# Residual kept feature-major in SBUF, expert layer norms by block transposes, routers in plain float32

## The chip, the cores and the metric

One core of one Trainium2 chip runs the whole program in one launch. The metric is the device time in microseconds. The kernel before took 512.14 us (median of 3 runs, 511.82 to 512.53).

## What is computed

A transformer block in float32 on x of shape (4, 512, 256): four batches of 512 tokens with 256 features. Cut to what matters:

```python
x = x + tanh(g_xattn) * attention(layernorm(x), ctx, ctx)   # 16 heads of 64, rope, window of 64
x = x + tanh(g_ffn)   * experts(layernorm(x))

def attention(q, k, v):             # per batch
    qh, kh, vh = rope(q @ wq.T), rope(k @ wk.T), v @ wv.T
    scores = where(window, qh @ kh.T * 64**-0.5, -1e30)
    return softmax(scores) @ vh @ wo.T

def experts(x):                     # 2 shared and 16 routed experts of width 128
    shared = sum(gelu(x @ up.T) @ down.T)
    probs = softmax(x @ router_w.T); gate = top 4 of probs, else 0
    routed = sum(gelu(x @ up.T) * gate @ down.T)
    return shared + routed
```

## The kernel before

All large products are made from float32r pairs: each operand is split into a high part (rounded by ScalarE, ACT) and a low part (the rest, subtracted by VectorE, DVE, or GpSimd, POOL), and `product` (L1126 to L1134) issues three matmuls on TensorE (PE) for a pair: high x high, high x low, low x high. In the names, xTh and xTl are the two parts of the normalised input with features on partitions, oTh and oTl those of the attention output (and of the experts' hidden values), wh and wl those of the weights, which come in pieces of 512 columns through four raw buffers.

The program runs in two phases. Attention goes through 16 units u (4 batches b of 4 groups g of 4 heads), and each unit through 4 chunks c, one per head; `steps` (L204 to L236) lists for each chunk the jobs that go with it: "q", "k", "v" project the next unit, "y" of unit u - 1 multiplies its attention output by wo and adds it to x, "w" fetches and splits a weight piece. Each engine walks the same list in order: PE makes scores, transposes probabilities and multiplies by v; DVE takes score maxima (L1026), inverts sums (L1036), makes the low parts (rest_att, L1040), rotates q and k (L856, L859), adds y (L962); ACT makes exponentials (L707) and copies; POOL does half of the rotation (L499 to L513), divides the probabilities (`divide`, L521) and makes some low parts of weights. The PSUM banks `ring[0]` and `ring[1]` alternate between the jobs q, k, v, y, xT and r.

x lies token-major, as (128 tokens, batch, 4 tiles, 256 features). For y the stationary operand is a tile of 128 tokens of oTh or oTl, and the moving operand is 256 columns of wo: 4 tiles x 2 head pairs x 3 = 24 matmuls (L1249 to L1258).

The expert phase runs through 4 x 18 steps n = (b, e): PE computes up(n) (6 matmuls of 512 columns into ring[0]) and down(n - 2) (6 matmuls; they accumulate over the 18 experts of a batch), ACT applies gelu (L616) and rounds (L632), DVE multiplies by the gate (`gated`, L921) and makes the low part (`rest_gated`, L929). `after` (L243 to L259) lists the extra jobs behind each expert: weight pieces in the first batch, and the preparation of the next batch.

That preparation, for the experts' layer norm of batch b: "stat" (DVE bn_stats L820, bn_aggr L823, L825, L826; POOL takes the power -0.5 at L555 and the shift at L556), "norm_a" and "norm_b" (ACT, L697) into xn; then for batches 0 and 1 "xT": PE transposes xn in 8 matmuls (L1219), ACT rounds the bank (L604, L606), DVE makes the low part (L804, L807). For batches 2 and 3 "turn": DVE transposes 32x32 blocks (L992), and 16 DMAs a time on SP's queue (`move`, L373) bring the blocks to their partitions; "xhi" and "xlo" split. Then "r" (router): batches 0 and 1 multiply a split router weight `rw_parts` by xTh and xTl in four matmuls of 512 columns (L1273), batches 2 and 3 (`FULL_ROUTER`) multiply in plain float32 in 8 matmuls of 128 columns (L1263). "rexp", "pick_a", "pick_b", "gT" and "spread" make the gates and broadcast them through DRAM. "back" turns x itself feature-major (L1005 and 16 DMAs), and "z" adds the experts' sum to it (L1014); the store follows. The layer norm ahead of attention uses for batches 0 and 1 the same token-major way, for batches 2 and 3 a second, feature-major input `in_xt` scaled on POOL (L540, L546).

What orders the work: on each engine the program's order, written out by hand, and semaphores between engines. After attention's steps a closing part (L1096 to L1117 on DVE, L1375 to L1393 on PE) mixes the last chunks with the first experts.

## Time and profile before

| | us |
|---|---|
| median of 3 runs | 512.14 |
| lowest, highest | 511.82, 512.53 |
| the profiled execution | 510.9 |
| its span in the profile | 509.1 |

Busy time is given for each engine: PE matmuls, PEld weight loads (beside the matmuls), DVE, ACT, POOL. In rows of a timeline the columns are the start, the duration, the engine, the line, the operation with its tiles and shapes, how many were merged, and in brackets the idle time of the engine just before with what ended it. Durations of neighbours on DVE and PE overlap, since an instruction begins while the one before drains: for a pace, starts are compared. Step 53 and the like are values of c.

### The profile page before, as it was taken

Reading aid. Unit: us, or ns where it says so; the run is one execution under the profiler, and the core shown is the slowest. Engines: PE = TensorE matmul, PEld = TensorE weight load, DVE = VectorE, ACT = ScalarE, POOL = GpSimd, SP = SyncE. Lnnn points to the kernel's source line nnn. Section 1 sums busy time; section 2 is a strip of 40 time slices with the busy share of each in tenths; the row PEclk is TensorE's granted clock in tenths of the full one; section 3 lists DMA queues with packets and bytes.
Section 4 is the critical chain, followed back from the end, with each engine's and each line's share of the span. In section 5 each row is a group of like instructions: output and inputs, shape, how many; then the busy total and the mean of one; then the engine's idle time right before and its main releaser. Section 6 shows DMA issues by size and latency. Waiting matters only on the chain.

```text
span 509.1 us, 12348 instructions
## 1 busy us (share of the span) xinstructions
PE 499.7 (98%) x4402; PEld 420.1 (83%) x4402; DVE 358.1 (70%) x1159; ACT 310.7 (61%) x861; POOL 266.8 (52%) x206
## 2 busy tenths in 40 slices
PE   8998999999999999999999999999999999999997
PEld 5788888889988998888888788777878887888885
DVE  6989958665787667767977777796657565745454
ACT  5596785656766665765876775766456545544442
POOL 4999999899997999997897511001000100000000
PEclk9999999999999999999999999999999999999999
DMA  7463224121123201220220147315701580256021
GB/s 264 120 203 65 58 69 131 43 80 38 46 75 78 62 27 34 57 58 9 74 59 23 38 138 259 103 27 169 251 14 29 151 266 14 32 144 241 1 34 49
DMA packets 49355, 46.23 MB, mean 91 GB/s; under 512 B 29936, under 2 KB 32368, under 8 KB 49296
## 3 DMA queue, kind: packets, MB, share of 16 engines
q1 hardware_dynamic: 49296, 45.46, 31.4%
q8 instruction: 35, 0.57, 0.5%
q14 instruction: 24, 0.20, 0.2%
HBM read 32.72 MB, written 2.24 MB: 69 GB/s over the span
## 4 chain that ended last, share of the span: by engine, by line
PE 79%; POOL 9%; DVE 5%; issue 3%; ACT 2%; DMA 1%; SPq 0%; DVEq 0%; POOLq 0%; ACTq 0%
PE ring L1131 56%; PE psS L1131 10%; PE psO L1341 5%; PE psS L1310 4%; PE psT L1322 4%; POOL prob L521 2%; POOL arena L508 2%; POOL arena L513 2%; DMA craw<-in_ctx 1%; POOL wl L529 1%; POOL arena L502 1%; DVE arena L859 1%; DVE arena L1026 1%; DVE wl L946 1%; DVE arena L856 1%
## 5 line engine op out<-in xcount | busy, mean ns | idle before, releaser
L1131 PE MATMUL ring<-xTh,wh 128*128 128x512 f32 x268 | 108.1, 403 | 0.3 <-DVE lex L888 0.2
L1131 PE MATMUL ring<-xTh,wl 128*128 128x512 f32 x268 | 105.2, 393 | 0.0
L1131 PE MATMUL ring<-xTl,wh 128*128 128x512 f32 x268 | 105.1, 392 | 0.0
L632 ACT ACTIVATE oTh<-prob 128x512 fp32r<-128x512 f32 x64 | 40.4, 632 | 54.4 <-PE ring L1131 26.8
L521 POOL TENSOR_TENSOR prob<-prob,rinv 128x512 f32<-128x512 f32 x62 | 66.7, 1076 | 13.0 <-DVE rinv L1036 12.9
L929 DVE TENSOR_TENSOR oTl<-prob,oTh 128x512 fp32r<-128x512 f32 x64 | 44.1, 689 | 37.1 <-ACT oTh L632 36.6
L555 POOL TENSOR_TENSOR rstd<-vare,mhalf 128x4 f32<-128x4 f32 x8 | 9.7, 1212 | 103.2 <-DVE vare L826 103.2
L616 ACT ACTIVATE sneg<-ring 128x512 f32<-128x512 f32 x72 | 42.9, 595 | 33.1 <-PE ring L1131 33.0
L921 DVE TENSOR_TENSOR prob<-sneg,arena 128x512 f32<-128x512 f32 x64 | 44.2, 690 | 24.8 <-ACT sneg L616 24.8
L1131 PEld LDWEIGHTS ring<-xTh,wh 128*128 128x128 f32 x268 | 50.3, 188 | 12.7 <-issue 0.9
L1131 PEld LDWEIGHTS ring<-xTh,wl 128*128 128x128 f32 x268 | 50.3, 188 | 11.1
L1131 PEld LDWEIGHTS ring<-xTl,wh 128*128 128x128 f32 x268 | 50.4, 188 | 10.4
L723 ACT ACTIVATE pT<-psT 128x512 f32<-128x512 f32 x64 | 38.0, 594 | 33.4 <-PE psT L1322 33.2
L707 ACT ACTIVATE prob<-arena,nmax 128x128 f32<-128x128 f32 x128 | 49.7, 394 | 10.9 <-DVE nmax L1026 10.8
L707 ACT ACTIVATE prob<-sneg,nmax 128x128 f32<-128x128 f32 x128 | 49.6, 391 | 6.8 <-DVE nmax L1026 6.7
L513 POOL TENSOR_TENSOR arena<-arena 128x512 f32<-128x512 f32 x37 | 48.9, 1322 | 2.7
L508 POOL TENSOR_TENSOR arena<-arena,sin 128x512 f32<-128x512 f32 x37 | 50.1, 1353 | 0.0
L856 DVE STREAM_SHUFFLE arena<-ring 128x512 f32<-128x512 f32 (+1 forms) x51 | 45.8, 897 | 0.2
L859 DVE TENSOR_TENSOR arena<-ring,cos 128x512 f32<-128x512 f32 (+1 forms) x51 | 41.3, 809 | 0.0
L729 ACT ACTIVATE oTh<-psO 128x512 fp32r<-128x512 f32 x32 | 19.1, 597 | 33.1 <-PE psO L1341 33.0
L962 DVE SCALAR_TENSOR_TENSOR x<-ring,tg,x 128x1024 f32<-128x1024 f32 x16 | 20.5, 1278 | 26.4 <-PE ring L1131 26.4
L1131 PE MATMUL ring<-wh,oTh 128*128 128x256 f32 x128 | 37.4, 292 | 1.5 <-DVE oTl L1040 1.4
(144 smaller groups left out, 1247.7 us busy)
## 6 DMA issues: line engine op xcount, KB each, us to landing
arena<-gate_scratch SPq DMA_DIRECT2D x64, 256.0 KB, 6.1
raw<-in_e SPq DMA_DIRECT2D x18, 256.0 KB, 2.6
raw<-in_w SPq DMA_DIRECT2D x16, 256.0 KB, 3.6
arena<-arena SPq DMA_DIRECT2D x16, 256.0 KB, 3.2
arena<-arena SPq DMA_DIRECT2D x16, 192.0 KB, 3.5
pT<-pT SPq DMA_DIRECT2D x96, 32.0 KB, 2.0
out<-x SPq DMA_DIRECT2D x16, 128.0 KB, 6.0
x<-in_x SPq DMA_DIRECT2D x3, 512.0 KB, 4.4
```

The source lines that it names most:

```text
L508: link(pool.tensor_tensor(part, part, sin[:, :], ALU.mult))
L513: pool.tensor_tensor(dst, dst, swap[:, i, pair, :], ALU.add).then_inc(qk_rot[i], 1)
L521: pool.tensor_tensor(prob[:, c % BUFS, :, :], prob[:, c % BUFS, :, :], rinv[:, c % BUFS, :].unsqueeze(2).to_broadcast([P, TT, P]), ALU.mul ...
L616: act.activation(act_g[:, n % 2, :], ring[0][:, n % 2, :], ACT.Gelu).then_inc(f_gelu, 1)
L632: act.activation(gated_parts(n)[0], src, ACT.Copy).then_inc(f_hi, 1)
L707: last = act.activation(prob[:, c % BUFS, t, :], sneg[c % BUFS][:, t, :], ACT.Exp, bias=nmax[:, c % 4, t:t + 1], scale=-1.0, accum_out=rsu ...
L723: act.activation(pT[:, c % 4, :, :], psT[:, :, :], ACT.Copy).then_inc(p_out, 1)
L856: dve.stream_shuffle(swap[:, i, pairs, :], part, [(lane + QUAD // 2) % QUAD for lane in range(QUAD)]).then_inc(qk_swap[i], 1)
L859: dve.tensor_tensor(dst[:, pairs, :], part, cos[:, :].unsqueeze(1).to_broadcast(part.shape), ALU.mult).then_inc(qk_mul[i], 1)
L921: dve.tensor_tensor(act_f[:, n % 4, :], act_g[:, n % 2, :], gate_bc[:, r, :], ALU.mult).then_inc(f_mul, 1)
L929: dve.tensor_tensor(lo, src, hi.bitcast(F32), ALU.subtract).then_inc(f_lo, 1)
L1131: last = pe.matmul(out, a, b, start=start and i == 0 and j == 0, stop=stop and i == n - 1 and j == 2, skip_group_check=check)
```

## The change

- x is kept feature-major, as (128 features, batch, 2 halves, 512 tokens), loaded from the second input `in_xt` for all batches (semaphores `in_xd`). The token-major copy goes only to xn, for the norm ahead of attention; ACT then normalises xn in place.
- y is computed with the weights stationary: 2 halves of features x 2 head pairs x 3 = 12 matmuls whose moving operand is 512 columns of oTh or oTl. z adds to x in place; "back" of before and all block moves by DMA go.
- The experts' layer norm works on x turned by 32x32 blocks: in such a tile each of 4 partition quadrants holds, for a block of 32 tokens, a quarter of the features along the free axis. Jobs, one batch at a time: "turn" (DVE transposes x into xn), "mean" (DVE reduces over two axes, copies the four quadrants' sums side by side, reduces them, spreads -mean to the quadrants in four operations), "centre" (POOL adds it, two operations), "square" (POOL, two), "var" (DVE, as mean, on the squares), "scale" (POOL: power -0.5 of 128x16, then two products), "back" (DVE transposes the blocks back). "xhi" and "xlo" split for all batches, and xT(4) and xT(5) go.
- For batch 0 these stand at steps 44 (turn), 46, 47, 51, 53 (var), 55, 57, 58 and 59; for the others behind experts e = 2 (turn), 3 (mean, centre), 4 (square), 5 (var), 6 (scale), 7 (back), 8, 9 of the batch before.
- All routers are in plain float32 (8 matmuls of 128 columns); `rw_parts` goes. The gates go to DRAM in four DMAs for every batch.

```diff
-            for e, kind in ((2, "turn"), (8, "xhi"), (9, "xlo"), (10, "r"), (11, "rexp"), (12, "pick_a"),
-                            (13, "pick_b"), (14, "gT")):
+        for b in range(B - 1):
+            for e, kind in ((2, "turn"), (3, "mean"), (3, "centre"), (4, "square"), (5, "var"), (6, "scale"), (7, "back"),
+                            (8, "xhi"), (9, "xlo"), (10, "r"), (11, "rexp"), (12, "pick_a"), (13, "pick_b"), (14, "gT")):
                 after[b * NE + e].append((kind, b + 1))
...
+            jobs += {44: [("turn", 0)], 46: [("mean", 0)], 47: [("centre", 0)], 51: [("square", 0)], 53: [("var", 0)],
+                     55: [("scale", 0)], 57: [("back", 0)], 58: [("xhi", 0)], 59: [("xlo", 0)]}.get(c, [])
...
                 elif kind == "q" and n % GROUPS == 0 and n // GROUPS + 1 < B:
                     b = n // GROUPS + 1
-                    sp.dma_start(x[:, b, :, :], x_d[b]).then_inc(in_x[b], 16)
+                    if b == 1:
+                        sp.dma_start(x[:, 0, :, :], xt_d[0]).then_inc(in_xd[0], 16)
+                        load_tokens(b)
+                    sp.dma_start(x[:, b, :, :], xt_d[b]).then_inc(in_xd[b], 16)
                     load_ctx(b)
...
+            def feature_norm(kind, n):
+                if kind == "centre":
+                    pool.wait_ge(f_mean, n + 1)
+                elif kind == "square":
+                    pool.wait_ge(f_centred, n + 1)
...
+                else:
+                    pool.wait_ge(f_var, n + 1)
+                    link(pool.tensor_tensor(rstd_d[:, :], vare_d[:, :], mhalf_d[:, :], ALU.pow))
+                for k in range(KC):
+                    half = xn_halves[:, k, :, :]
+                    if kind == "square":
+                        flat = xd[:, k, :]
+                        last = pool.tensor_tensor(turned(n)[:, k, :], flat, flat, ALU.mult)
+                    else:
+                        values, op = (nmean_d, ALU.add) if kind == "centre" else (rstd_d, ALU.mult)
+                        last = pool.tensor_tensor(half, half, per_block(values), op)
...
+            def over_features(halves):
+
+                link(dve.tensor_reduce(part[:, :], halves.rearrange("p k m d -> p m k d"), AX_XY, ALU.add))
+                for a in range(4):
+                    last = dve.tensor_copy(four[:, :, a], part[QUAD * a:QUAD * (a + 1), :])
+                link(last)
+                link(dve.tensor_reduce(total[:, :], four[:, :, :], AX_X, ALU.add))
...
+                elif kind == "mean":
+                    over_features(xn_halves)
+                    for a in range(4):
+                        last = dve.tensor_scalar(nmean_d[QUAD * a:QUAD * (a + 1), :], total[:, :], -1.0 / D, None,
+                                                 ALU.mult)
+                    last.then_inc(f_mean, 1)
+                elif kind == "var":
+                    dve.wait_ge(f_squared, n + 1)
+                    over_features(turned(n).rearrange("p k (m d) -> p k m d", m=BLOCKS))
...
+                elif kind == "back":
+                    dve.wait_ge(f_scaled, n + 1)
+                    dve.transpose(turned(n).rearrange("p k n -> p (k n)"), xn_flat).then_inc(f_turned, 1)
...
-                    for t in range(TT):
-                        last = product(two[t // 2][:, (t % 2) * D:(t % 2 + 1) * D],
-                                       [(oTh[:, j, t * P:(t + 1) * P], oTl[:, j, t * P:(t + 1) * P])
-                                        for j in range(2)],
-                                       [cols(i, j * D, D) for j in range(2)])
+                    for kc in range(KC):
+                        last = product(two[kc], [cols(i, j * D + kc * P, P) for j in range(2)],
+                                       [(oTh[:, j, :], oTl[:, j, :]) for j in range(2)])
```

## Rows read from the trace of the kernel before

**Rows 1.** The page: busy us, share of the span and instructions.

```profile
PE 499.7 (98%) x4402; PEld 420.1 (83%) x4402; DVE 358.1 (70%) x1159; ACT 310.7 (61%) x861; POOL 266.8 (52%) x206
```

**Rows 2.** Busy time by stretch, then granted clock, DMA share, GB/s.

```profile
30.00:87.00 57.00, 54.67 (x683) 47.90 (x685) 46.59 (x175) 42.61 (x147) 55.90 (x43) 1.00 0.36 94
300.00:340.00 40.00, 40.00 (x216) 32.23 (x214) 30.04 (x63) 26.13 (x47) 1.70 (x2) 1.00 0.50 159
```

**Rows 3.** The chain of waits: start, us, what (k, then y).

```profile
109.44 2.76 PE ring L1131 x12
...
118.26 2.88 PE ring L1131 x24
```

**Rows 4.** Timeline of PE: transposes of xT(4), and a plain router.

```profile
281.60 1.03 PE L1219 MATMUL ring<-ident,xn 128*128 128x128 f32 x8
282.47 0.60 PE L1322 MATMUL psT<-ident,prob 128*128 128x128 f32 x4
...
381.04 0.63 PE L1263 MATMUL psT<-pT,rw 128*16 128x128 f32 x16
381.60 0.50 PE L1131 MATMUL ring<-xTh,wh 128*128 128x512 f32 x1
```

**Rows 5.** Timeline of DVE in the closing chain.

```profile
284.65 1.22 DVE L804 TENSOR_TENSOR xTl<-ring,xTh 128x1024 fp32r<-128x1024 f32 x1 [1.48 <-ACT xTh L604]
285.80 0.28 DVE L1026 CUSTOM_DVE_ANT_0 sneg<-psS,mask 128x128 f32<-128x128 f32 x1
```

**Rows 6.** Groups by line and shape: busy us, mean ns, idle before.

```profile
L521 POOL TENSOR_TENSOR prob<-prob,rinv 128x512 f32<-128x512 f32 x62 | 66.7, 1076 | 13.0 <-DVE rinv L1036 12.9
L508 POOL TENSOR_TENSOR arena<-arena,sin 128x512 f32<-128x512 f32 x37 | 50.1, 1353 | 0.0
L555 POOL TENSOR_TENSOR rstd<-vare,mhalf 128x4 f32<-128x4 f32 x8 | 9.7, 1212 | 103.2 <-DVE vare L826 103.2
L1005 DVE STREAM_TRANSPOSE pT<-x 128x1024 f32<-128x1024 f32 x4 | 5.0, 1239 | 0.0
L556 POOL TENSOR_TENSOR shift<-nmean,rstd 128x4 f32<-128x4 f32 x8 | 1.9, 232 | 0.6
L895 DVE TENSOR_REDUCE lsum<-lexp 128x4 f32<-128x64 f32 x4 | 0.9, 214 | 0.0
```

**Rows 7.** Timeline of POOL and of DVE, at 244.86 us.

```profile
244.86 1.29 POOL L508 TENSOR_TENSOR arena<-arena,sin 128x512 f32<-128x512 f32 x1
...
244.87 1.31 DVE L825 TENSOR_SCALAR nmean<-mv 128x4 f32<-128x4 f32 x1
```

**Rows 8.** Timeline of DVE and PE around the y jobs after steps 53 and 57.

```profile
260.22 0.65 DVE L1040 TENSOR_TENSOR oTl<-psO,oTh 128x512 fp32r<-128x512 f32 x1
...
261.02 0.36 PE L1131 MATMUL ring<-wh,oTh 128*128 128x256 f32 x1 [0.25 <-DVE oTl L1040]
...
277.22 0.67 DVE L1040 TENSOR_TENSOR oTl<-psO,oTh 128x512 fp32r<-128x512 f32 x1
...
278.29 0.60 PE L1322 MATMUL psT<-ident,prob 128*128 128x128 f32 x4
```

**Rows 9.** Timeline of DVE (after step 46) and POOL (after step 55).

```profile
227.97 1.28 DVE L962 SCALAR_TENSOR_TENSOR x<-ring,tg,x 128x1024 f32<-128x1024 f32 x1 [2.91 <-PE ring L1131]
...
269.04 1.04 POOL L521 TENSOR_TENSOR prob<-prob,rinv 128x512 f32<-128x512 f32 x1 [2.40 <-DVE rinv L1036]
```

**Rows 10.** Timeline of DVE and PE in an undisturbed expert step of batch 1.

```profile
363.68 0.69 DVE L921 TENSOR_TENSOR prob<-sneg,arena 128x512 f32<-128x512 f32 x1 [0.59 <-ACT sneg L616]
365.17 0.69 DVE L929 TENSOR_TENSOR oTl<-prob,oTh 128x512 fp32r<-128x512 f32 x1 [0.81 <-ACT oTh L632]
...
368.41 0.40 PE L1131 MATMUL ring<-oTh,wh 128*128 128x512 f32 x1
```

**Rows 11.** Timeline of DVE and PE in batch 0: weight piece 3, down(5).

```profile
310.83 0.68 DVE L946 TENSOR_TENSOR wl<-raw,wh 128x512 fp32r<-128x512 f32 x1
...
318.86 0.40 PE L1131 MATMUL psS<-oTh,wh 128*128 128x512 f32 x1
```

More of the change, by code:

```diff
@@ L95, in build @@
         rw = sb("rw", [P, KC, NR])
[L96 removed]
+        part = sb("part", [P, BLOCKS])
+        four = sb("four", [QUAD, BLOCKS, 4])
+        total = sb("total", [QUAD, BLOCKS])
+        nmean_d = sb("nmean_d", [P, BLOCKS])
+        vare_d = sb("vare_d", [P, BLOCKS])
+        rstd_d = sb("rstd_d", [P, BLOCKS])
+        mhalf_d = sb("mhalf_d", [P, BLOCKS])
         sizes = dict(swap=(2, 2, L), qT=(2, 2, L), kT=(2, 2, W + L), idle=(1, 1, L), late=(2, TT, P), spare=(1, 1, 256),
@@ L157, in build @@
         in_const = sem("in_const")
+        in_xd = [sem(f"in_xd{b}") for b in range(B)]
         idle_set = sem("idle_set")
@@ L315, in side, with turned @@
             return 0 if j < B else (j - B) % 2
-        def gates_stored(b):
-            return 16 * sum(TT if n in FULL_ROUTER else 1 for n in range(b + 1))
+        def turned(n):
+            return craw[:, :, :] if n == 0 else pT[:, 0:2, :, :].rearrange("p k t c -> p k (t c)")
         def wait_w_lo(eng, i):
@@ L406, in _ @@
                 part = slice(2 * half, 2 * half + 2)
-                sp.dma_start(x[:, 0, part, :], x_d[0][:, part, :]).then_inc(in_x0[half], 16)
+                sp.dma_start(xn[:, part, :], x_d[0][:, part, :]).then_inc(in_x0[half], 16)
             load_piece(0)
@@ L455, in do @@
                     spread_gates(n)
-                elif kind == "turn":
-                    sp.wait_ge(xn_turned, n - 1)
-                    move(x1_blocks, xn_blocks, xn_moved)
-                elif kind == "back":
-                    sp.wait_ge(x1_turned, n + 1)
-                    move(xn_blocks, x1_blocks, x1_moved)
                 elif kind == "z":
@@ L1091, in _ @@
                 for job in jobs:
-                    if (c, job[0]) == (CLOSING - 2, "xT"):
+                    if (c, job[0]) == (CLOSING - 2, "xlo"):
                         invert(CLOSING - 2)
@@ L1263, in do @@
                             last = pe.matmul(two[0][QUAD * t:QUAD * t + NR, 0:P], rw[:, kc, :],
-                                             xnT[:, kc, t * P:(t + 1) * P], start=kc == 0, stop=kc == KC - 1)
-                    last.then_inc(r_pe, 1)
-                elif kind == "r":
-                    pe.wait_ge(rw_lo, 1)
-                    pe.wait_ge(xT_lo, B + n + 1)
-                    X = side(B + n)
-                    for kc in range(KC):
-                        for part in (xTh[X], xTl[X]):
-                            last = pe.matmul(two[0][0:2 * NR, :], rw_parts[:, kc, :, :].rearrange("p a e -> p (a e)"),
-                                             part[:, kc, :], start=kc == 0 and part is xTh[X],
-                                             stop=kc == KC - 1 and part is xTl[X])
+                                             turned(n)[:, kc, t * P:(t + 1) * P], start=kc == 0, stop=kc == KC - 1)
                     last.then_inc(r_pe, 1)
```

206 lines of the change are left out of this document (84 added, 122 removed).

## The prediction

> **What bounds the kernel now.** I read the busy shares first [rows 1]: TensorE (PE) 98%, VectorE (DVE) 70%, ScalarE (ACT) 61%, GpSimd (POOL) 52%. A mean over stages hides limits, so I read the busy time by stretch [rows 2]. From 30 to 87 us POOL is busy 55.90 of 57 us and PE idles between jobs: this stretch is bound by POOL. From 87 us to the end PE is busy all the time, and the granted clock is 1.00 throughout (the 2.4 GHz level), so the end is set by PE's own instructions plus every stall of PE. POOL is nearly full until 290 us and almost empty in the expert phase. The question for each edit is therefore: does it take instructions off PE after 87 us, and does it put something on DVE or POOL that PE then waits for?
>
> **What comes off PE.** Sixteen y jobs go from 24 products of 256 columns to 12 of 512. In the chain of waits an undisturbed y is a piece of 24 products in 2.88 us, 0.120 each, and a q or k job, which has the form that y is to get, 12 products in 2.76 us, 0.230 each [rows 3]. A job gains 0.12 to 0.13 us. y 0 to 2 run before 87 us, where POOL binds, and give nothing; 13 x 0.13 = 1.7 us. The Trainium skill ("TensorE: Matmul & The Clock Gate", Back-to-back issue gap) has the gap as columns / 2.4 plus 2.5 ns, which would be 109 and 216 ns, and a saving of only 0.03 us a job; the rows give 0.120 and 0.230, so the halved number of instructions is worth more here. By the page the sum below would be 1.3 us longer.
>
> Two transpose jobs xT(4), xT(5) go: eight transposes take 281.60 to 282.47, 0.87 us each job [rows 4]. Routers 0 and 1 change from four products of 512 columns (4 x 0.23 = 0.92 us) to the plain form, which takes 0.56 us (381.04 to 381.60) [rows 4]: 0.36 us each. In the closing chain (282 to 291 us) PE also waits for DVE: the low part of xT(4) can't start until ACT has read the bank (DVE idle 1.48 us), score_max(60) starts behind it at 285.80 [rows 5], scores(62) wait for that, and the first up waits for the router's subtraction. After the change xhi is long done, the low part follows the y addition at once, score_max starts about 1.1 us earlier, and the router has one transpose on DVE in place of four and an addition. I take 1.65 us for this whole chain, the 0.87 and 0.36 of its own PE work among it. Outside it 0.87 + 0.36 remain for batch 1, and a stall of 0.27 us in batch 0 that the statistics of batch 1 cause (they go). Gains: 1.7 + 1.65 + 1.23 + 0.27 = 4.85 us.
>
> ACT loses 16 normalisations and gains one rounding, the 96 small moves of SP's queue go, SP gains two 512 KB loads and some gate stores. Of these I expect nothing, since DMA is busy 0.36 of the time from 30 to 87 us and 0.50 from 300 to 340 [rows 2], and a weight piece is asked for four pieces ahead; the first y additions now wait for x itself, asked for some 25 us earlier. Without this cover a load would cost its few us of landing. SP's order has new waits only for reads of xn that are past by then. In the POOL-bound stretch the change adds no POOL work but a tiny memset: zero.
>
> **What is put on DVE and POOL.** For each batch: turn (a 1024-element transpose, 1.24 us), mean, centre (2 POOL), square (2 POOL), var, scale (POOL power and 2 products), back (1.24), then xhi and xlo as before. No row shows a two-axis reduction of 1024 elements. Below: a reduction of 64 elements takes 0.21 us; above: a transpose of 1024 takes 1.24 us [rows 6]. I take 1.2 us, by the row of the same size; the far ends are 0.6 and 2.4, half and double its pace. With four small copies and four small tensor_scalars (estimated at 0.1 each, overlapping, from the small reduction's 0.21), the second reduction (0.21) and three links, mean or var costs 2.35 us on a free DVE.
> POOL: the product with a broadcast operand takes 1.08 us in the mean, with two full operands 1.35, queueing included [rows 6]; free of it I count 1.04 and 1.28: centre 2.1, square 2.55, the two scalings 2.1. The power takes 1.2 us on 4 columns, and a product of the same shape 0.23 [rows 6]. So 0.8 to 1.0 us is the power itself, and I can't see whether it is a fixed cost (then 1.2 us for 16 columns) or one per column (0.2 + 4 x 0.82 = 3.5 us). I take 3.5, since the product's time too follows its columns (0.23 for 4, 1.08 for 512) once a small start is paid.
> A lock between the two engines is in the rows: a tiny tensor_scalar of DVE took 1.31 us, though a larger reduction takes 0.21, and ended just as the POOL product beside it did (244.86 + 1.29) [rows 7]. The Trainium skill ("SBUF — State Buffer", Who interferes with whom) says that copies and tensor_scalars lock the port pair only in a two-port mode, so the short strided copies of mean and var may escape it; by that a var beside a busy POOL would cost 2.35 us and not the value I use.
>
> **In attention (batch 0's norm).** DVE's order decides. From the k rotation to the low part of the attention output it has no gap: rotation, weight piece, score maxima, reciprocal, oTl from 260.22 on, and y starts at 261.02, when oTl is there: PE already waits for it (0.25 us idle), with no slack left [rows 8].
> - var is put in just there (step 53). It delays score_max(54) and oTl by its whole length: 2.35 us, and one POOL operation's wait of about 1.25: 3.6 us, all on PE. Bounds 2.35 and 4.9 (both groups of small operations wait).
> - turn (step 44) precedes the same kind of DVE run: of its 1.24 us about 0.8 is idle time of DVE before the rotations; 0.4 us reach PE.
> - mean (step 46) lies in DVE's wait for y (2.91 us idle [rows 9], and slack behind it): 0. If that cover were short it would cost up to 1 us.
> - back (step 57): oTl ends at 277.22 + 0.67 now, and y follows the transposes of 278.29, which take 0.35 us [rows 8]; 1.24 later oTl is 0.5 us too late, 0.55 with the signal.
> - centre, square and scale on POOL: there are holes of this size, as the 2.40 us before the division at 269.04 [rows 9], square takes the place of the old statistics' power, and scale has besides the hole what PE loses to var: 0. Without the holes scale alone would cost up to 3 us.
> Loss: 3.6 + 0.4 + 0.55 = 4.55 us (2.9 to 6.5).
>
> **In the expert phase.** The pitch is 2.78 us a step. In an undisturbed step DVE ends gated(n) at 364.3 (363.68 + 0.6, its pace), starts the low part of n at 365.17, and down(n) starts at 368.41 [rows 10]. Whatever DVE does between them fits if it is shorter than 368.41 - 364.3 - 0.7 = 3.4 us. Mean (2.35) fits. But var waits for the squares: from the end of mean POOL needs one wait for the low part (0.65), 2.1 + 2.55 = 4.65 us, and about 1.0 us of waits for the lock, then var 2.35, the low part 0.65. up(n) ends two steps before down(n), at 362.85, and gated(n) begins 0.83 us after it. Counted from the end of up(2), gated(3) begins at 2.78 + 0.83 = 3.6, mean ends at 3.6 + 0.6 + 2.35 = 6.55, so the low part of 5 is there at 6.55 + 0.65 + 4.65 + 1.0 + 2.35 + 0.65 = 15.85, and down(5) is due at 5 x 2.78 = 13.9: 1.95 us of stall, in batches 2 and 3 alike: 3.9 (0.9 to 2.95 each).
> For batch 1 (during the experts of batch 0) DVE also makes weight pieces and comes out of y(15) late: its piece at 310.83, so mean runs 311.45 to 313.8. The same sum, with 1.3 us for the lock, gives 323.4, against 318.86 less the old 0.27 for down(5) [rows 11]: 4.8 us (3.3 to 6).
> back waits for scale: from the end of var 3.5 + 2.1 + 0.1, then 1.24 + 0.65 = 7.6 us, and down(7) is due 6.25 us after it (0.7 for down(5), which waited, and two steps): 1.35 us in each of three batches, 4.05. With the cheap power there is none.
> Loss: 3.9 + 4.8 + 4.05 = 12.75 us.
>
> **Sum.** 4.55 + 12.75 - 4.85 = +12.45 us. The profiled execution took 510.9 us (span 509.1 and 1.8 around it): 523.4. The median of the runs shown, 512.1, is 1.2 above it, which gives 524.6; I say 524.0.
>
> **Rivals.**
> A. Forecast, 524.0: chance 0.34.
> B. The power costs 1.2 us whatever its columns: less 4.05, 520.0. For it: its time hardly resembles that of a product of four columns. Chance 0.26.
> C. Faster, the other side: mechanism, the norm's chain is shorter than my rows say (reduction near 0.6 us, POOL and DVE interleave without queueing), so that var meets its squares inside the 3.4 us of room. Then only var's and the others' 1.9 us in attention and 1.5 us of batch 0 stay, 3.4 against 4.85, with the median 510.7. It decides where the time from the start of mean to the end of var falls under some 8.2 us. Chance 0.21 for faster; 0.06 more ends within 0.2% (1 us, about what a measurement of this kernel can tell from no change).
> D. The two-axis reduction, whose input is read in two separate pieces, costs two cycles an element: 1.2 us more in attention, and 2.2 to 2.4 in each of three batches: 531. Chance 0.13.
> The change doesn't do what it says (the y products gain nothing): 1.7 us more in any case, inside the range. The range 510.5 to 531 leaves out the lower half of C and the tail of D. Faster by over 0.2%: 0.21, same 0.06, slower 0.73.
>
> **What would show it.** The y products start 0.229 us apart. A reduction row of 128x1024 near 1.2 us; a power row of 128x16 near 3.5 us; PE's longest stalls at the y job after step 53 (about 3.6 us), before down(5) and down(7) of each of the first three batches of experts, each put down to oTl of DVE. POOL has its rows in three bursts after 310 us. The prediction is wrong if PE shows no stalls there, if the reductions are short, or if a stall that I put at 0 (the closing chain's queue, the gates of batch 0, POOL's divisions after scale) appears.

## The result, and the profile after

| | before | after |
|---|---|---|
| median, us | 511.98 | 534.62 |
| span of the profiled execution, us | 509.1 | 532.7 |
| mean granted clock of TensorE | 1.00 | 0.983 |

The medians are of six runs each (for before, the three of the table further up and three more). The runs of after lie between 534.29 and 535.63. The ratio is 1.0447 (95% interval 1.0433 to 1.046): the kernel became 22.6 us slower. The prediction was 12 us slower, with 531.0 as its upper end. The direction was right, the size was not.

The page of after, busy us with share of the span, then the granted clock in 40 slices of 13.3 us:

```profile
PE 505.9 (95%) x4218; PEld 412.4 (77%) x4218; DVE 379.6 (71%) x1185; ACT 303.1 (57%) x843; POOL 305.8 (57%) x227
...
PEclk9999999999999999999979998899989999999999
```

PE fell from 98% to 95% [rows 1], so it stands still for more than before. The busy us themselves rose from 499.7 to 505.9, although PE has fewer instructions: part of them ran at a lower clock, in the slices with a 7 or 8.

The same two stretches as in [rows 2]:

```profile
30.00:87.00 57.00, 54.16 (x622) 45.62 (x620) 44.34 (x176) 42.94 (x148) 55.97 (x43) 1.00 0.43 125
300.00:340.00 40.00, 35.41 (x198) 27.47 (x197) 31.46 (x76) 20.78 (x47) 13.60 (x9) 0.91 0.45 146
```

The POOL-bound stretch hasn't changed. From 300 to 340 us PE, which had been busy for all 40 us, is busy for 35.41, and its mean clock is 0.91. POOL has 13.60 us of work there in place of 1.70.

The new groups, which answer to [rows 6] (busy us, mean ns, idle before):

```profile
L560 POOL TENSOR_TENSOR rstd_d<-vare_d,mhalf_d 128x16 f32<-128x16 f32 x4 | 13.1, 3286 | 10.2 <-DVE vare_d L1007 10.2
L893 DVE COPY four<-part 32x16 f32<-32x16 f32 x32 | 10.2, 319 | 0.6
L996 DVE STREAM_TRANSPOSE xn<-x 128x1024 f32<-128x1024 f32 x4 | 4.9, 1237 | 0.0
L891 DVE TENSOR_REDUCE part<-xn 128x16 f32<-128x1024 f32 x4 | 4.9, 1213 | 0.0
```

Power 3.29 us, transpose 1.24, reduction 1.21: the three sizes on which the forecast stood were right (3.5, 1.24, 1.2). The copies were not: 319 ns in the mean, where 100 had been put down.

Attention, around the variance at step 53. First DVE, then PE (start, us; in brackets the idle time before and its releaser):

```profile
259.98 1.21 DVE L891 TENSOR_REDUCE part<-craw 128x16 f32<-128x1024 f32 x1
261.21 2.54 DVE L893 COPY four<-part 32x16 f32<-32x16 f32 x4
263.79 0.21 DVE L895 TENSOR_REDUCE total<-four 32x16 f32<-32x64 f32 x1
264.03 0.70 DVE L1007 TENSOR_SCALAR vare_d<-total 32x16 f32<-32x16 f32 x4
264.76 0.29 DVE L1036 CUSTOM_DVE_ANT_0 arena<-psS,mask 128x128 f32<-128x128 f32 x1
...
266.54 0.66 DVE L1050 TENSOR_TENSOR oTl<-psO,oTh 128x512 fp32r<-128x512 f32 x1
```

```profile
261.73 0.60 PE L1312 MATMUL psT<-ident,prob 128*128 128x128 f32 x4
267.35 0.77 PE L1137 MATMUL ring<-oTh,wh 128*128 128x512 f32 x1 [5.02 <-DVE oTl L1050]
267.92 0.63 PE L1137 MATMUL ring<-oTl,wh 128*128 128x512 f32 x1
268.34 0.63 PE L1137 MATMUL ring<-oTh,wl 128*128 128x512 f32 x1
...
272.61 0.64 PE L1312 MATMUL psT<-ident,prob 128*128 128x128 f32 x4
```

In [rows 8] the same y waited 0.25 us; now it waits 5.02, for `oTl` of DVE, which is late because the variance (259.98 to 264.7) stands ahead of it and takes 4.7 us. Then comes what the forecast doesn't have at all: the 12 products start 0.427 us apart instead of 0.230, and the job takes 5.26 us (267.35 to 272.61) where an undisturbed one takes 2.81. The windows over it name the cause (granted clock in the third last column):

```profile
266.00:268.00 2.00, 0.65 (x2) 0.58 (x3) 1.38 (x9) 2.00 (x9) 1.29 (x2) 0.50 0.00 0
268.00:270.00 2.00, 2.00 (x6) 1.57 (x5) 0.00 (x0) 2.00 (x9) 1.92 (x2) 0.50 0.32 68
270.00:272.00 2.00, 2.00 (x6) 1.56 (x5) 0.00 (x0) 0.30 (x2) 2.00 (x3) 0.50 0.61 162
272.00:274.00 2.00, 2.00 (x36) 1.53 (x37) 1.15 (x1) 0.72 (x2) 2.00 (x1) 0.83 0.00 0
```

TensorE had stood 5 us, and the chip granted it the 1.2 GHz level (0.50) until about 272.7.

Experts, the norm of batch 2 (timelines of DVE, of POOL and of PE):

```profile
376.13 1.21 DVE L891 TENSOR_REDUCE part<-xn 128x16 f32<-128x1024 f32 x1
377.37 0.73 DVE L893 COPY four<-part 32x16 f32<-32x16 f32 x4
...
379.72 1.54 DVE L926 TENSOR_TENSOR prob<-sneg,arena 128x512 f32<-128x512 f32 x1
...
385.10 1.22 DVE L891 TENSOR_REDUCE part<-pT 128x16 f32<-128x1024 f32 x1 [0.94 <-POOL pT L565]
...
388.08 0.69 DVE L934 TENSOR_TENSOR oTl<-prob,oTh 128x512 fp32r<-128x512 f32 x1
```

```profile
379.16 3.01 POOL L568 TENSOR_TENSOR xn<-xn,nmean_d 128x512 f32<-128x512 f32 x2 [41.21 <-DVE nmean_d L1000]
382.25 2.82 POOL L565 TENSOR_TENSOR pT<-xn 128x512 f32<-128x512 f32 x2
388.13 3.41 POOL L560 TENSOR_TENSOR rstd_d<-vare_d,mhalf_d 128x16 f32<-128x16 f32 x1 [3.06 <-DVE vare_d L1007]
```

```profile
388.83 0.79 PE L1137 MATMUL ring<-oTh,wh 128*128 128x512 f32 x1 [2.83 <-DVE oTl L934]
389.42 0.63 PE L1137 MATMUL ring<-oTl,wh 128*128 128x512 f32 x1
```

This is the forecast's picture: DVE reaches the variance, stands 0.94 us until POOL's squares are there, and the low part that down(5) needs is queued behind it. PE stops for 2.83 us, and again goes on at 0.43 us a product; the eighth product after the first starts at 392.29, 3.46 us later instead of 1.85: 1.6 us.

Summed over the run, the waits of PE for DVE (us in total, times, longest):

```profile
PE psS L1137 <- DVE oTl L934: 8.3, 4, 2.8
PE ring L1137 <- DVE oTl L1050: 7.2, 5, 5.0
...
PE ring L1137 <- DVE oTl L934: 2.8, 1, 2.8
```

The long ones are listed here with the time that is lost from the start of one product to the start of the next, which is 0.1 to 0.3 us more than the wait itself: y after step 53, 5.3 us (about 0.5 of it was there before); down(4) 2.17 and down(5) 2.74 in batch 1; down(5) 2.99 in batch 2 and in batch 3; down(7) 1.09 in batch 3. The products that follow at the half level lost 2.45 us in the y and 1.55, 1.56 and 1.6 us in the experts, 7.2 in all. Behind down(5) of batch 3 nothing was lost: the clock stayed at 1.00. In batch 1 the level fell only about 1 us after PE had gone on (granted clock 0.99 from 322.88 to 323.88, 0.50 in the three us that follow), so the slow products aren't always the first ones.

### The profile page after: what moved, and what is told of

It is laid out like the page before. It is cut to its first block, busy times and chain, and to the rows that moved or that the text cites. A ratio compares the mean times of both kernels' runs of the same rounds, so it can differ in the third digit from the quotient of the medians.

```text
span 532.7 us, 11908 instructions
## 1 busy us (share of the span) xinstructions
PE 505.9 (95%) x4218; PEld 412.4 (77%) x4218; DVE 379.6 (71%) x1185; ACT 303.1 (57%) x843; POOL 305.8 (57%) x227
## 4 chain that ended last, share of the span: by engine, by line
PE 51%; issue 21%; DVE 14%; POOL 9%; ACT 2%; DMA 1%; POOLq 0%; SPq 0%; DVEq 0%; ACTq 0%
PE ring L1137 35%; PE psO L1331 4%; PE psS L1300 4%; PE psS L1137 3%; PE psT L1312 3%; DVE arena L864 2%; POOL xn L568 2%; POOL rstd_d L560 2%; DVE four L893 2%; DVE arena L861 1%; POOL prob L502 1%; DVE arena L1036 1%; PE psS L1154 1%; DVE part L891 1%; DVE wl L951 1%
## 5 line engine op out<-in xcount | busy, mean ns | idle before, releaser
L1137 PE MATMUL ring<-xTh,wh 128*128 128x512 f32 x268 | 109.9, 410 | 0.1
L1137 PE MATMUL ring<-xTl,wh 128*128 128x512 f32 x268 | 106.2, 396 | 0.0
L502 POOL TENSOR_TENSOR prob<-prob,rinv 128x512 f32<-128x512 f32 x62 | 68.3, 1102 | 11.7 <-DVE rinv L1046 11.6
L568 POOL TENSOR_TENSOR xn<-xn,nmean_d 128x512 f32<-128x512 f32 x8 | 11.1, 1405 | 99.2 <-DVE nmean_d L1000 99.2
L1137 PE MATMUL ring<-oTh,wh 128*128 128x512 f32 x136 | 56.9, 418 | 10.2 <-DVE oTl L1050 7.2
L926 DVE TENSOR_TENSOR prob<-sneg,arena 128x512 f32<-128x512 f32 x64 | 49.2, 769 | 19.8 <-ACT sneg L629 19.8
L1137 PEld LDWEIGHTS ring<-xTh,wl 128*128 128x128 f32 x268 | 51.0, 190 | 11.9
L1137 PE MATMUL ring<-oTh,wl 128*128 128x512 f32 x136 | 55.2, 406 | 0.0
L1137 PE MATMUL ring<-oTl,wh 128*128 128x512 f32 x136 | 55.0, 405 | 0.0
```

The source lines that it names most:

```text
L502: pool.tensor_tensor(prob[:, c % BUFS, :, :], prob[:, c % BUFS, :, :], rinv[:, c % BUFS, :].unsqueeze(2).to_broadcast([P, TT, P]), ALU.mul ...
L926: dve.tensor_tensor(act_f[:, n % 4, :], act_g[:, n % 2, :], gate_bc[:, r, :], ALU.mult).then_inc(f_mul, 1)
L1137: last = pe.matmul(out, a, b, start=start and i == 0 and j == 0, stop=stop and i == n - 1 and j == 2, skip_group_check=check)
```

## The experiments

The theory after this reading: (1) the whole loss is PE standing still for DVE, because the norm's steps are put where DVE has no room or before what they wait for is there, plus the half-level clock after such stalls; the rest of the change is a gain. The rivals: the other parts of the change cost something themselves; POOL's power, or DVE's total load, is the bound wherever the steps stand.

**The norm's arithmetic left out.** Mean, centring, square, variance and scaling are gone, so that the experts and routers get x itself; turn, back and both parts stay. A third part of the edit, not shown, gives back the waits that the square had for its buffers.

```diff
-    jobs += {44: [("turn", 0)], 46: [("mean", 0)], 47: [("centre", 0)], 51: [("square", 0)], 53: [("var", 0)],
-             55: [("scale", 0)], 57: [("back", 0)], 58: [("xhi", 0)], 59: [("xlo", 0)]}.get(c, [])
+    jobs += {44: [("turn", 0)], 57: [("back", 0)], 58: [("xhi", 0)], 59: [("xlo", 0)]}.get(c, [])
...
-    (2, "turn"), (3, "mean"), (3, "centre"), (4, "square"), (5, "var"), (6, "scale"), (7, "back"),
+    (2, "turn"), (7, "back"),
...
```

> Leaves out mean, centre, square, var and scale of the experts' layer norm (the blocks are turned and turned back; the experts get x unnormalised). Theory 1 (the norm's work on DVE and POOL stalls PE, 16.7 us, and the granted clock falls behind three or four of these stalls, 7 us more): all of it goes, 532.7 - 24 = about 509 us of span, 0.995 to 1.00 of the kernel before. Theory 2 (the new y form, the wider loads or the place of the work in the program cost it): over 515 us stays.

Measured: 509.76 us, ratio 0.9962 (0.9947 to 0.9977). PE has no wait longer than 0.40 us after 200 us, and its clock is 1.00 in every stretch of 10 us up to 500. So the norm's arithmetic in its places costs 24.9 us (534.62 - 509.76), and everything else, turn and back included, brings 2.3 us. The first rival is out.

One cost of the forecast can be read here by itself, that of back at step 57. The y behind it, first in before, then in this kernel:

```profile
278.64 0.37 PE L1131 MATMUL ring<-wh,oTh 128*128 128x256 f32 x1
```

```profile
279.68 0.47 PE L1142 MATMUL ring<-oTh,wh 128*128 128x512 f32 x1 [0.30 <-DVE oTl L1055]
```

From the start of the transposes ahead of it (278.29 and 278.79) it is 0.35 and 0.89 us: back costs 0.54. In v2 below, where back stands at step 58, the same distance is 0.36 again.

**The variance one step later** (54 instead of 53).

```diff
-    51: [("square", 0)], 53: [("var", 0)],
+    51: [("square", 0)], 54: [("var", 0)],
```

> var of batch 0 one step later, behind the low part of the attention output, in DVE's wait for y. Theory 1: the 5.3 us that PE waits before the y after step 53 shrink to the 0.5 us of before, and the twelve products behind it run at 0.23 us instead of 0.43: 6 us less, at most 7.3 (up to 1.5 us may come back, since var beside POOL takes 4.7 us and the wait has room for about 3). Rival (the stall only moves, to scale, back or the closing part): 0 to 2 us less.

Measured: 532.25 us, ratio 1.0402 (1.0384 to 1.0419), 2.4 us less than after and not 6. The 5 us wait of y is gone, and so is its half-level clock, but PE now waits 1.83 and 1.77 us for POOL's divisions, because power and scaling come to stand among them with POOL full:

```profile
PE psT L1312 <- POOL prob L502: 4.5, 5, 1.8
```

The stall and its slow products, 4.8 and 2.45 us, are gone and 2.4 us are won. In the profiled execution, 530.97 us, 3.5 us less than that of after, the two waits for POOL account for the 3.6 us that came back, and the clock stayed at 1.00 behind both. The other three runs take 532.15 to 533.34 us, two of them at a mean clock of 0.984 instead of 0.990; what else came back in them no trace shows. The rival was nearer than the theory.

**PE kept busy during the wait**: 22 products whose result is overwritten, before y(12), in the time in which PE stands still anyway.

```diff
+    if n == 12:
+        for _ in range(22):
+            pe.matmul(two[0], wh[:, slot(i), 0:P], wh[:, slot(i), :], start=True, stop=True)
```

> Twenty-two products of 0.23 us (5.0 us) that PE throws away, ahead of its wait for the low part before the y after step 53; nothing else changes. Theory 1 with the clock as a cost of its own: the wait ends when it did, but the granted clock stays at 1.00, and the y takes 2.8 instead of 5.5 us: 2.5 us less. Rival (the slow y is the reading of fresh operands or the queue, not the clock): 0, or up to 0.5 us more.

Measured: 532.46 us, ratio 1.0398 (1.0381 to 1.0415). The wait is as long as before, only filled, and y behind it runs at full speed. PE and windows of this kernel:

```profile
262.76 5.26 PE L1257 MATMUL ring<-wh 128*128 128x512 f32 x22
267.99 0.51 PE L1137 MATMUL ring<-oTh,wh 128*128 128x512 f32 x1
268.33 0.39 PE L1137 MATMUL ring<-oTl,wh 128*128 128x512 f32 x1
```

```profile
264.00:268.00 4.00, 4.00 (x19) 3.02 (x17) 3.78 (x25) 1.55 (x8) 0.83 (x2) 1.00 0.00 0
268.00:272.00 4.00, 4.00 (x37) 3.23 (x40) 1.08 (x2) 3.51 (x13) 3.92 (x4) 1.00 0.45 111
```

2.2 us are won by work that does nothing. That the slow products are a second price of the stall, paid after it, is shown by this.

The same trace shows how this price is tied to the next stall. In batch 2 of this kernel PE stood 2.83 us as in after, but the clock stayed at 1.00, and here the wait before down(7) appears, which after has in batch 3 alone:

```profile
393.77 0.50 PE L1137 MATMUL ring<-oTh,wh 128*128 128x512 f32 x1 [0.92 <-DVE oTl L934]
```

From down(5) of batch 2 to down(5) of batch 3 it is 55.51 us in after, with slow products and no wait before down(7), and 55.18 here, with the wait and no slow products. Of the 1.6 us that slow products took there, a full clock gives back only 0.3 in these two executions.

**The power replaced by a product** (the scale factor is then not the reciprocal root).

```diff
-    link(pool.tensor_tensor(rstd_d[:, :], vare_d[:, :], mhalf_d[:, :], ALU.pow))
+    link(pool.tensor_tensor(rstd_d[:, :], vare_d[:, :], mhalf_d[:, :], ALU.mult))
```

> The power of the variance (3.3 us on 16 columns) replaced by a product (about 0.2 us), so the norm's scale is wrong. Theory 1 as the trace of the changed kernel has it: back is late for PE only in batch 3 (0.9 to 1.1 us before down(7)): 1.1 us less, and the waits before down(5) stay at 2.8 us. Rival, the step of the blind forecast: 1.35 us in each of three batches, 4 us less.

Measured: 533.24 us, ratio 1.0415 (1.0399 to 1.043): 1.4 us. PE loses 2.74, 2.97 and 2.97 us before down(5), as with the power; only the one before down(7) in batch 3 went. The profiled execution is 1.8 us shorter than that of after; 1.1 of it is this wait, and 0.8 is luck with the clock, since the y behind its unchanged stall lost 1.63 us in slow products instead of 2.45, while in the experts they took 4.8 as against 4.7. In batch 2 the clock stayed at 1.00 here too, and without the power there is no wait before down(7), where the kernel that keeps PE busy has 0.92. So the power's 3.3 us, which the forecast had at 4.05 us on the path, cost 1.1: a PE that has just stood 3 us and then runs slowly gives POOL the time.

**The small copies as reductions** of one element each.

```diff
-    last = dve.tensor_copy(four[:, :, a], part[QUAD * a:QUAD * (a + 1), :])
+    last = dve.tensor_reduce(four[:, :, a], part[QUAD * a:QUAD * (a + 1), :].unsqueeze(2), AX_X, ALU.add)
```

> The four small copies that gather the quadrants' partial sums on DVE become one-element reductions of the same 32x16 elements; nothing else changes. Theory 1 (copies share the lock with POOL, reductions don't): four cost 0.7 to 0.9 us in attention too, where the copies took 2.54 (variance) and 3.65 us (mean). PE's stall after step 53 shrinks from 5.3 to about 3.5 us; with the half-level products behind it that is 2 to 4 us off the time of after, 531 to 532.5 us. In the experts nothing changes beyond 0.5 us. Rival (DVE is slowed by POOL whatever the operation): the four reductions take 2.5 us or more, and the time stays within 1 us of after, 534 to 535.

Measured: 533.54 us, ratio 1.0418 (1.0394 to 1.0442), 1.1 us less than after. That isn't clear of noise: its four runs lie between 532.46 and 534.84, those of after begin at 534.29, and the two intervals overlap. What the trace shows doesn't hang on it. DVE at the variance:

```profile
260.66 0.72 DVE L893 TENSOR_REDUCE four<-part 32x16 f32<-32x16 f32 x4
261.42 0.21 DVE L896 TENSOR_REDUCE total<-four 32x16 f32<-32x64 f32 x1
261.66 1.35 DVE L1008 TENSOR_SCALAR vare_d<-total 32x16 f32<-32x16 f32 x2
```

Four copies take 0.73 us where POOL is idle (377.37), 2.54 beside it here, and 3.65 in the mean of attention (226.93); four reductions take 0.72 beside a busy POOL. The lock is real for the copies and absent for the reductions. But the wait moved into the four tensor_scalars behind them, which took 1.7 us together instead of 0.70, and 2.81 in the mean of attention. In the mean the copies of after (226.93 + 3.65) and the tensor_scalars of this kernel (227.94 + 2.81) end within 0.2 us of the end of POOL's run of three products (230.53 and 230.55): the first group that needs what POOL holds waits until POOL pauses. The stall of y fell only from 5.3 to 4.5 us. And the clock took some back: in this execution the half level followed the stall of batch 3 too, where it cost 2.84 us, and there the wait before down(7) is gone.

```profile
443.00:447.00 4.00, 3.91 (x9) 3.13 (x10) 1.96 (x4) 1.75 (x3) 3.92 (x3) 0.50 0.01 2
```

The Trainium skill ("SBUF — State Buffer", Who interferes with whom) has these forms as the runs show them: a reduction never contends with GpSimd, a copy or a tensor_scalar can, and a tensor_tensor with both inputs in SBUF contends with its reads. The last is seen in the experts, where the product at 379.72 took 1.54 us beside POOL and takes 0.69 alone.

**The experts' order alone shifted later.**

```diff
-    (3, "mean"), (3, "centre"), (4, "square"), (5, "var"), (6, "scale"), (7, "back"),
-    (8, "xhi"), (9, "xlo"), (10, "r"), (11, "rexp"), (12, "pick_a"), (13, "pick_b"), (14, "gT")
+    (3, "mean"), (3, "centre"), (4, "square"), (7, "var"), (8, "scale"), (11, "back"),
+    (12, "xhi"), (12, "r"), (13, "rexp"), (13, "xlo"), (14, "pick_a"), (15, "pick_b"), (15, "gT")
```

> Only the order of the experts' steps changes against after: variance behind step 7 instead of 5, scale 8, back 11, high part and router 12, exponential and low part 13, gates 14 and 15. Engines and arithmetic stay. Theory 1 (the stalls are DVE standing in the variance's wait for POOL's squares ahead of the low part that PE needs, and the half-level clock follows from them): the stalls before down(4), down(5) and down(7) go, 12.0 us, and their half-level products, 4.7 us: 534.6 - 16 = about 518.5 us (516 to 521). Rival (POOL's chain itself is late or DVE is too full, so that the stall goes to whatever step stands behind the variance or to the next batch's gates): less than 8 us gained, 527 us or more.

Measured: 523.78 us, ratio 1.0231 (1.0213 to 1.0249): 10.8 us gained, with every instruction kept. The stalls before down(5) are gone; behind the moved variance, before down(8), PE waits 0.29 us in batches 2 and 3 and 0.96 in batch 1. What I missed is batch 1: its 2.02 us before down(4) stand where they stood, since the mean at step 3 causes them, behind the y addition and a weight piece, and the mean had not been moved; a half level (0.67 from 323 to 327 us) follows them. The rival (less than 8 us) is out, the theory was 5 us too hopeful.

**Another placement (v2)**: copies as reductions, both reductions in steps of their own, centring and scaling on DVE, the square on ACT, only the power on POOL.

```diff
+    jobs += {44: [("turn", 0)], 46: [("sum_m", 0), ("mean", 0)], 50: [("centre", 0)], 51: [("square", 0)],
+             54: [("sum_v", 0), ("var", 0)], 55: [("pow", 0)], 58: [("scale", 0), ("back", 0)],
+             59: [("xhi", 0), ("xlo", 0)]}.get(c, [])
...
+    (2, "turn"), (3, "sum_m"), (4, "mean"), (5, "centre"), (6, "square"), (7, "sum_v"), (8, "var"), (8, "pow"),
+    (10, "scale"), (11, "back"), (12, "xhi"), (12, "r"), (13, "rexp"), (13, "xlo"), (14, "pick_a"), ...
+    act.activation(turned(n), xd, ACT.Square).then_inc(f_squared, 1)
```

> The same sums by another placement: the gathering copies as reductions; each norm reduction split in two steps of the order; centre and scale on DVE, square on ACT, and only the power left on POOL; in attention the variance one step later and the scaling behind step 58; in the experts every step of the chain later, the variance at step 8, scale at 10, back at 11. Theory 1 (the 22.6 us are PE's stalls for DVE, where the chain DVE-POOL-DVE is not given time, and the half-level clock behind them; the arithmetic itself fits beside the products): all stalls over 1 us in the experts go, in attention at most 2 us stay, the clock is 1.00 nearly throughout: 510 to 514 us. Rival (DVE has no room for the work, wherever it stands): with 8 more full-width products on DVE for each batch, some 9 us each, the stalls only move, 522 us or more.

Measured: 513.44 us, ratio 1.0034 (1.002 to 1.0049), 21.2 us less than after with the same norm computed. DVE is busier than in after (383.6 us instead of 379.6), so its load was never the bound. In the experts no wait of PE is over 0.49 us. One loss is left, at the end of attention: PE waits for a division of POOL, and in the profiled execution the half level follows. Two of the seven runs, 513.09 and 512.78 us, have a mean clock of 1.00, the other five 0.995 to 0.997.

```profile
287.01 0.66 PE L1341 MATMUL psT<-ident,prob 128*128 128x128 f32 x4 [1.79 <-POOL prob L505]
```

```profile
288.00:290.00 2.00, 1.78 (x30) 1.25 (x24) 0.48 (x2) 2.00 (x10) 0.00 (x0) 0.69 0.00 0
290.00:292.00 2.00, 2.00 (x40) 1.67 (x34) 1.29 (x6) 1.86 (x9) 1.04 (x1) 0.50 0.03 8
```

**v2 with the original copies** (the line of the diff above taken back).

> The version of v2 with the original copies in the gathering of the quadrants. Theory 1 (the lock costs only where POOL is busy beside it): in attention the copies before y after step 54 take 1.5 to 3 us instead of 0.7, in the experts the same 0.7 since POOL is idle there: 1 to 3 us over v2. Rival: no lock on the copies: within 0.5 us of v2.

Measured: 515.16 us, ratio 1.0065 (1.0044 to 1.0085), 1.7 us over v2, inside the 1 to 3 expected, though the runs of the two overlap (514.00 to 515.97 against 512.78 to 515.03). Beside POOL the four copies of the variance take 3.64 us instead of 0.73. Most of these 2.9 us is no gain of the reductions, because the tensor_scalars behind them take it over; in v2:

```profile
263.63 2.81 DVE L1036 TENSOR_SCALAR vare_d<-total 32x16 f32<-32x16 f32 x4
```

With the copies these take 0.70. The whole group is 5.05 us long in v2 and 5.85 in this version, and the mean in attention differs by as much: twice 0.8 us, which is about the 1.7 measured.

**Three attempts to remove the last wait.** v3 takes v2's chain earlier:

```diff
+    48: [("centre", 0), ("square", 0)], 50: [("sum_v", 0), ("var", 0)], 51: [("pow", 0)],
+    54: [("scale", 0), ("back", 0)], 58: [("xhi", 0)], 59: [("xlo", 0)]
```

> v2 with the attention part of the chain moved earlier: centre and square at step 48, the variance at 50, the power at 51, scale and back at 54; high and low part stay at 58 and 59. In the trace of the version without the norm POOL idles 2.40 us before the division at 251.57 and 1.05 us before the rotation at 253.66, and has no gap from 271.71 to 286; v2 has its power at 267.7 and its scaling beside POOL's last rotations. Theory 1 (the power costs PE nothing if it stands in holes of POOL, and DVE's scaling nothing if no POOL result is late then): PE's wait of 1.79 us for POOL's division at 287 and the slower products behind it go, 1.5 to 3 us off v2: 510.5 to 512. Rival (the steps 48 and 50 have no room on DVE, the loss comes back as waits of y or scores there): 513 or more.

Measured: 520.20 us, ratio 1.0146 (1.0122 to 1.0171), 6.8 us worse than v2, by neither of the mechanisms named. ACT, and PE behind it:

```profile
242.43 1.06 ACT L699 ACTIVATE craw<-xn 128x1024 f32<-128x1024 f32 x1 [7.07 <-DVE xn L1024]
...
244.12 1.09 PE L1341 MATMUL psT<-ident,prob 128*128 128x128 f32 x4 [5.78 <-ACT pT L746]
```

I had put the square in the same step as the centring that it waits for. The centring, beside POOL's rotation products of 2.4 and 2.7 us, took from 237.7 to 242.4; ACT stood in the square's wait with the evictions queued behind it, PE stood 5.78 us, and a granted clock of 0.50 for about 6 us came with that. It is the mistake of the change itself, on another engine.

v4 takes the variance as the mean of the squares less the square of the mean, so that the square waits for nothing recent. v5 is v4 with the scaling back at 58.

```diff
+    link(dve.tensor_tensor(four[:, :, 0], nmean_d[0:QUAD, :], nmean_d[0:QUAD, :], ALU.mult))
+    link(dve.scalar_tensor_tensor(total[:, :], total[:, :], 1.0 / D, four[:, :, 0], ALU.mult, ALU.subtract))
...
+    49: [("square", 0)], 50: [("sum_v", 0), ("var", 0)], 51: [("pow", 0)], 54: [("centre", 0), ("scale", 0)],
+    58: [("back", 0)], 59: [("xhi", 0), ("xlo", 0)]
```

> v2 with the variance as the mean of the squares less the square of the mean, so that the squares don't wait for the centring. In v3 ACT stood 7.07 us in the square's wait for the centring of the same step, PE 5.78 us behind it; here the square (step 49) reads only what has been ready since step 46, the variance is at step 50, the power at 51, centring and scaling both on DVE at 54, back at 58; the experts' order is v2's, with the square at 5 and the centring at 9. Theory 1 (a step costs nothing where what it waits for is long there, and PE's loss in v2 is the queue on POOL at 282 to 287): the wait of 1.79 us for POOL's division goes, no new one over 1 us: 510.5 to 512.5, at or below before. Rival (any 3 us of work on DVE at step 54 puts y or scores late, since the order has no room left): 513 to 516.

> v4 with the scaling back at step 58, the centring alone at 54. In v4 centring and scaling at step 54 took DVE 6.5 us (263.35 to 269.85) beside a busy POOL, the reciprocal and the rotations behind them came 1.75 us later than in the version without the norm, POOL's chain (275.5 to 290.5 without a gap) kept that delay, and PE waited 1.80 us for its division. Theory 1 (DVE's steps of over 4 us are what puts POOL's chain late): with some 3.2 us at step 54 and 4.5 at 58, as in v2, and the power out of the way at 51, PE's wait for the division falls under 1 us: 511.5 to 513.5. Rival (the work of the norm beside a busy POOL costs its lock time wherever it stands, some 3 to 4 us over the version without the norm): 513.5 to 516.

Measured: v4 515.67 us, ratio 1.0067 (1.0052 to 1.0082); v5 514.12 us, ratio 1.0046 (1.0029 to 1.0064). The wait of PE for ACT is gone in both, but the one for POOL's division is still there, 1.80 us in both, and in the profiled executions the half level behind it (four of the six runs of v4 have a mean clock of 1.00). The timeline of v5, and its window:

```profile
287.88 0.80 PE L1346 MATMUL psT<-ident,prob 128*128 128x128 f32 x4 [1.80 <-POOL prob L505]
```

```profile
288.00:290.00 2.00, 2.00 (x22) 1.19 (x23) 1.22 (x7) 1.28 (x6) 0.82 (x1) 0.57 0.00 0
```

So it isn't the power's place that makes this wait: with the power at 51 it is as long as at 55. Nor is it the scaling's, which stands at 54 in v4 and at 58 in v5: that the wait falls under 1 us in v5 is out. For both kernels the rival's range held (513 to 516 and 513.5 to 516). DVE's products with two SBUF operands are slow beside a full POOL (the two of v2's scaling take 3.19 us at 278.30, two of the same form 1.29 in the experts); that they are what puts POOL's division late is not shown, and which operation makes the 1.80 us was not told apart. The version without the norm waits 0.40 us at this place. None of the versions with the norm is faster than before; v2 is nearest, 0.34% slower, and its interval overlaps that of v5.

## Why the prediction was off

| term of the sum, us | forecast | measured |
|---|---|---|
| gains (y, xT, routers, closing chain, old stall) | -4.85 | -2.85 |
| variance at step 53 | 3.6 | 4.8 |
| turn, back and mean in attention | 0.95 | 1.15 |
| batch 1 (down(4), down(5)) | 4.8 | 4.9 |
| batches 2 and 3, down(5) | 3.9 | 6.0 |
| back, down(7) | 4.05 | 1.1 |
| products at the half level | 0 | 7.2 |
| sum | 12.45 | 22.3 |

The measured column is from the stalls and products read above, the first line from the version without the norm (2.3 us gained, with back's 0.54 in it); the third is this 0.54 and what y lost more at 243.13, after step 49. Its sum is within 0.3 us of the 22.6 between the medians.

**The step that failed** is the one that isn't in the sum: the prediction took the clock as 1.00 throughout because the trace of before has 1.00 throughout, while the change that it costed was to make PE stand 2 to 5 us several times. Before has no stall of that length after 87 us, so its trace couldn't say what follows one. It had to be bounded: below by nothing, above by one job of 2.8 us at double length behind each of the four waits that I put at 1.95 us or more, 11 us, and the upper end would have been 542. Without the 7.2 us the measured time would lie at 527.4, inside the range. But 7.2 us is what the slow products took and not what a full clock would have saved: it would have brought back waits before down(7), as batch 2 of the kernel that keeps PE busy shows, where 1.6 us of slow products were exchanged for 0.92 us of wait and the stretch became 0.3 us shorter. The Trainium skill ("TensorE: Matmul & The Clock Gate", Part 1) names the two levels, and the trace agrees with 0.50 and 1.00. What the Trainium skill puts there below 1% of a typical kernel's span is the penalty of the ramp when matmul work sets in, which is no price for stalls later in a kernel; here the slow products behind them take 7.2 of 534.6 us, 1.3%.

**Gains, 2.0 us too high.** The y pieces fell from 2.88 to 2.81 us, 0.07 each and not 0.13. The row of k that I had taken, 2.76, has the same form but another pace: in both jobs the second product starts 0.32 us after the first, but the later ones of y are 0.234 us apart and those of k 0.229. Why is not shown. That is 0.8 of the 2.0 us. The closing chain has little part in it: from the end of the y behind step 57 to the transposes before the next y it is 10.76 us in before (281.60 to 292.36) and 9.33 in the version without the norm (282.57 to 291.90), 1.4 us gained where 1.65 were forecast. Most of what is left was lost earlier: at 278 us that version is 0.5 us behind before, 0.3 of it already at 100 us, and what costs this is open. The chain of waits of after:

```profile
101.44 2.81 PE ring L1137 x12
...
110.21 2.75 PE ring L1137 x12
```

**Attention.** The variance's mechanism was right, its size 1.2 us too low: the variance takes 2.95 us on a free DVE and not 2.35, and where one wait of 1.25 us for POOL had been put down, the copies waited 1.8 us. They did not escape the lock, as the prediction had thought possible. Back came out by its term, 0.54 us against 0.55. Turn, put at 0.4, cost nothing that I can find: the y behind it starts 0.72 us after its transposes in after, 0.69 in before. The mean, put at 0, cost 0.6: with reductions for its copies the loss at 243.1 is what it is without the norm (0.48 us).

**Batches 2 and 3, 1.05 us too low each.** Mean and variance take 2.95 us on a free DVE, not 2.35: the four copies take 0.73 and the four tensor_scalars 0.70, where 0.4 each had been put down with overlap, and the links between them cost some too. Both stand in the chain of that stall, so the error counts twice. The structure of the chain, its end and its queue came out as written; POOL's centring and square took 5.9 us (379.16 to 385.07), where the sum has 0.65 + 4.65 + 1.0.

**Batch 1** came out by its sum, but in two stalls: the mean too was late, before down(4).

**back, 3 us too high.** I had counted the wait before down(7) as if PE ran on at full speed from down(5). In batches 1 and 2 PE ran at half speed behind the stall, which gave POOL and DVE the time; only in batch 3, with the clock at 1.00, the wait came, 1.09 us against 1.35. Two other kernels show the same exchange the other way round: where PE is kept busy, batch 2 kept 1.00 and had the wait, with reductions for copies batch 3 fell to 0.50 and had none. Two terms of a sum were not independent.

**Rivals.** B (the power has a fixed cost) is out by its row, 3.29 us; but so is A's use of it, since the version without the power gained 1.4 us and not 4. C (a short chain) is out by its own sign: from the start of the mean to the end of the variance it is 11.9 us in batch 2 (376.13 to 388.05), not under 8.2. D (a slow reduction) is out by the reduction's row, 1.21 us.

## What to carry to other kernels

Price a stall of TensorE by what follows it as well: where a change makes it stand a few us, one job behind the stall may run at 1.2 GHz, and the sum needs that as a term with a range from nothing, even though the trace of before shows a clock of 1.00; and what PE loses there can cover a later wait, so the two aren't simply added. In a hand-written order of one queue per engine, place a step by when its input is ready, not by when its output is wanted: the order alone was worth 10.8 us, another split of the work among the engines and placement 21.2, at the same arithmetic. Beside a busy GpSimd, count the first short copy or tensor_scalar on VectorE as lasting until GpSimd pauses, which can be several of its operations (3.65 us here). A reduction in its place doesn't wait, but the gain is small where such an operation follows it: 0.8 us of the 2.9 here.

## What the runs showed of the hardware

- A stall doesn't always cost the clock: in batch 3 of after PE stood 2.83 us and went on at 1.00, in batch 2 it stood 2.83 us and went on at 0.50; in the kernel with reductions for copies batch 3 got 0.50 as well. Waits of 1.83 and 1.77 us for POOL's divisions (variance one step later) left the clock at 1.00, one of 1.79 in v2 was followed by 0.50. The length of the stall alone doesn't decide it.
- At the half level the products of 512 columns start 0.427 us apart, at the full one 0.229 (k) to 0.234 (y).
- The power of POOL takes 1.21 us for 128x4 and 3.29 for 128x16: by an estimate from these two sizes alone, 0.17 us for each further column, with about 0.52 to start.
- A small copy of 32x16 takes 0.18 us alone and 0.6 to 0.9 in the mean beside POOL (2.54 to 3.65 us for four); the same elements by a reduction 0.18 in either case. Four tensor_scalars of 32x16 take 0.70 us alone and up to 2.82 beside POOL.
